# A build-time planner is told about the port that VectorE and GpSimd share, and two of its duration formulas are refitted

## What is computed

```python
def block(x):                                   # x: 2048 x 256
    q, k, v = split(layernorm(x) @ Wqkv.T + b)   # 8 query pairs, 4 key pairs, 4 values of 256
    p1 = softmax(causal(q[:, 0] @ k[:, 0].T * D**-0.5))
    p2 = softmax(causal(q[:, 1] @ k[:, 1].T * D**-0.5))
    o = (p1 - lam * p2) @ v
    o = o * rsqrt(mean(o * o) + eps) * subln_w * (1 - LAMBDA_INIT)
    x = x + layernorm(concat_heads(o) @ out_w.T + out_b)
    h = fwht(x * SU_ug) / 64
    h = silu(h @ W_gate.T * ws_g) * (h @ W_up.T * ws_u)
    return x + layernorm((fwht(h * SU_dp) / 64) @ W_down.T * ws_d)
```

## Time and profile before

| what | value |
|---|---|
| runs | 1252.57 us median of 3 (1249.90 to 1254.59) |
| profiled execution | 1250.54 us |
| its span, first to last instruction | 1248.7 us |
| busy PE / DVE / ACT / POOL | 1194.9 (96%) / 993.0 (80%) / 984.4 (79%) / 833.3 (67%) us |
| mean granted TensorE clock | 0.995 of full speed |

### The profile page before, as it was taken

One profiled execution on the slowest core, in us unless ns is written; L12 is line 12 of the kernel. 1 busy time (PEld: TensorE's weight loads), 2 busy tenths in 40 slices (PEclk: granted clock), 3 DMA queues, 4 the chain that ended last, 5 costly groups with the idle time before them and its releaser, 6 DMA issues.

```text
span 1248.7 us, 26399 instructions
## 1 busy us (share of the span) xinstructions
PE 1194.9 (96%) x8102; PEld 1010.6 (81%) x8102; DVE 993.0 (80%) x2492; ACT 984.4 (79%) x2617; POOL 833.3 (67%) x1167
## 2 busy tenths in 40 slices
PE   8899999999999999999999999999988899999998
PEld 7787888888878888888888888889777678777887
DVE  6888888888778988889689988887778899837445
ACT  4788988988789888888689889887887789856341
POOL 3576776666666776767577776566569887875542
PEclk9999999999999999999999999999999999999999
DMA  3255554463266556542555554543645455530001
GB/s 132 63 83 103 90 97 93 90 113 69 49 119 110 96 90 92 103 78 52 124 90 96 89 96 89 100 77 69 112 90 100 93 99 103 120 60 2 29 18 38
DMA packets 368153, 106.62 MB, mean 85 GB/s; under 512 B 359312, under 2 KB 365712, under 8 KB 367504
## 3 DMA queue, kind: packets, MB, share of 16 engines
q1 hardware_dynamic: 366672, 103.37, 44.4%
q10 hardware_dynamic: 1344, 1.57, 0.4%
HBM read 14.71 MB, written 2.10 MB: 13 GB/s over the span
## 4 chain that ended last, share of the span: by engine, by line
PE 49%; DVE 20%; POOL 11%; ACT 9%; issue 7%; DMA 3%; SPq 1%; ACTq 0%; POOLq 0%; DVEq 0%
PE score_bank L1181 6%; DVE p L1460 6%; PE score_bank L1047 5%; PE score_bank L1053 4%; DVE mx L1449 4%; PE score_bank L1050 4%; POOL e_all L1733 4%; ACT e_all L1220 4%; PE turn_bank L1074 2%; PE turn_bank L1076 2%; PE turn_bank L1075 2%; DVE score_bank L1444 2%; PE turn_bank L1091 2%; PE turn_bank L1127 2%; PE turn_bank L1146 2%
## 5 line engine op out<-in xcount | busy, mean ns | idle before, releaser
L1220 ACT ACTIVATE e_all<-score_bank,negmx 128x512 f32<-128x512 f32 (+2 forms) x640 | 395.4, 629 | 40.1 <-DVE negmx L1453 27.0
L1733 POOL TENSOR_TENSOR e_all<-e_all 128x512 f32<-128x512 f32 (+3 forms) x320 | 375.8, 1190 | 41.2 <-ACT e_all L1235 32.2
L1047 PE MATMUL score_bank<-k_hi,q_hi 128*128 128x512 f32 (+2 forms) x640 | 254.8, 398 | 27.2 <-ACT e_all L1220 16.3
L1460 DVE SCALAR_TENSOR_TENSOR p<-e_all,gain,p 128x512 f16<-128x512 f32 (+3 forms) x320 | 257.8, 821 | 17.6 <-ACT p L1242 17.3
L1449 DVE TENSOR_REDUCE mx<-score_bank 128x1 f32<-128x512 f32 (+1 forms) x384 | 242.1, 637 | 28.6 <-PE score_bank L1053 27.8
L1242 ACT ACTIVATE p<-e_all,gain 128x512 f16<-128x512 f32 (+3 forms) x320 | 206.8, 673 | 37.0 <-POOL e_all L1733 36.2
L1050 PE MATMUL score_bank<-k_lo,q_hi 128*128 128x512 f32 (+2 forms) x640 | 231.5, 362 | 0.4 <-DVE k_lo L1510 0.4
L1053 PE MATMUL score_bank<-k_hi,q_lo 128*128 128x512 f32 (+2 forms) x640 | 231.6, 362 | 0.0
L1784 POOL TENSOR_SCALAR ratio<-s,inv,neg_lam 128x1 f32<-128x1 f32 x128 | 55.9, 437 | 175.5 <-DVE inv L1721 175.0
L1047 PEld LDWEIGHTS score_bank<-k_hi,q_hi 128*128 128x128 f32 x640 | 120.8, 189 | 64.4 <-ACT e_all L1220 31.3
L1074 PE MATMUL turn_bank<-v,p16T 128*128 128x256 f16 x592 | 163.0, 275 | 0.0
(11 more groups left out here) (384 smaller groups left out, 2822.0 us busy)
## 6 DMA issues: line engine op xcount, KB each, us to landing
p16T<-p SPq DMA_TRANSPOSE x320, 3.1
w_raw<-in_w_qkv_dram SPq DMA_DIRECT2D x3, 1024.0 KB, 5.5
w_raw<-in_w_o_dram SPq DMA_DIRECT2D x4, 512.0 KB, 3.2
oT<-o SPq DMA_TRANSPOSE x128, 2.5
bv<-in_hidden_dram SPq DMA_DIRECT2D x8, 256.0 KB, 3.1
w_raw<-in_w_ug_dram SPq DMA_DIRECT2D x4, 512.0 KB, 3.6
out_dram<-e SPq DMA_DIRECT2D x16, 128.0 KB, 1.7
e<-in_w_d_dram SPq DMA_DIRECT2D x1, 1024.0 KB, 6.0
```

The lines of the kernel that those rows point to most:

```text
L1047: pe.matmul(bank[:, 0:w], qh, kh, start=True, stop=False)
L1220: act.activation(e, S[k % NS][:, 0:w], ACT.Exp, bias=negmx[:, d % 2, m, s:s + 1], scale=-1.0 if alone else 1.0, accum_out=ssum[:, d % 4, s ...
L1460: dve.scalar_tensor_tensor(out=halves_of(q, w)[1], in0=e1_of(q, w), scalar=gain[:, d % 4, s:s + 1], in1=halves_of(q, w)[0], op0=ALU.mult, ...
L1733: pool.tensor_tensor(a, a, b, ALU.add).then_inc(p_pool, 1)
```

## The change

In words, in the order of the diff:

1. PE durations in the plan. A score set of `w` columns goes from `0.00136 * w + 0.01` to `0.00135 * w + 0.003`; a product chunk from `0.00257 * w + 0.02` to `0.002555 * w`; the 0.083 us that the plan added to a score set behind a product or an output (`SWITCH_US`, with the list `ran`) is gone.
2. POOL durations. `MIX` goes from `0.19 + 0.00212 * w` to `0.22 + 0.00198 * w`, `VL` from 1.3 to 1.15.
3. A port in the simulation. `BOTH_FROM_SBUF` names the DVE steps that read two tensors from SBUF (the `SPLIT` of a chunk, weight splits, `FH`, `DB`); `LONG_ON_POOL` names the long POOL steps. A listed DVE step started while a long POOL step runs is charged the rest of that step; any POOL step started during a listed DVE step is charged the rest of that one.
4. A choice. A listed DVE step is left out of the candidates while the long POOL step that runs still needs 0.3 us or more (`HELD_SHORT`), unless it has been ready for over 6 us (`HELD_LONG`).
5. `FB` 0 to 3 may not start in the plan until SP's `WO` of the last group plus 5 us; SP's `FB` steps get a line of their own ("DF" for "D").
6. One instruction stream changes directly: ACT waits, ahead of `SQ` of tile `o`, for its own `SQ` of tile `o - 2`.

```diff
-LOAD_LAG, SWITCH_US, TURN_LAG = 0.16, 0.083, 2.9
-SCORE_US, VALUE_US = 0.00136, 0.00257
+LOAD_LAG, TURN_LAG = 0.16, 2.9
+SCORE_US, VALUE_US = 0.00135, 0.002555
+BOTH_FROM_SBUF = ("SPLIT", "WQ", "WK", "WV", "WO", "FH", "DB")
+LONG_ON_POOL = ("MIX", "VL", "FB", "NA", "HH", "DB")
+HELD_SHORT, HELD_LONG = 0.3, 6.0
...
-    ran = ["X"]
+    port, ready_at = {"DVE": 0.0, "POOL": 0.0}, {}
...
-                        add("M", "POOL", "MIX", (d, jj), 0.19 + 0.00212 * ww, [("POOL", "GAIN", o)], 2)
+                        add("M", "POOL", "MIX", (d, jj), 0.22 + 0.00198 * ww, [("POOL", "GAIN", o)], 2)
...
-            add("V", split, "VL", what, 0.75 if split == "DVE" else 1.3, [("ACT", "V", what)], 1)
+            add("V", split, "VL", what, 0.75 if split == "DVE" else 1.15, [("ACT", "V", what)], 1)
...
-            add("D", "SP", "WO", what, 0.3, [("DVE", kind, what)], 1)
+            add("D", "SP", "WO", what, 0.3, [("DVE", kind, what)], 1, 5.0)
...
-            loaded = [("SP", "FB", what // 2 * 2 - 3)] if what >= 4 else []
+            loaded = [("SP", "FB", what // 2 * 2 - 3)] if what >= 4 else [("SP", "WO", (GROUPS - 1, s)) for s in range(2)]
...
-            add("D", "SP", kind, what, 0.3, [("POOL", kind, what)], 1, 5.0 if what in (1, 3) else 0.0)
+            add("DF", "SP", kind, what, 0.3, [("POOL", kind, what)], 1, 5.0 if what in (1, 3) else 0.0)
...
-            return SCORE_US * duo_chunks(what[0])[what[1 + 1]][4] + 0.01
+            return SCORE_US * duo_chunks(what[0])[what[1 + 1]][4] + 0.003
         if kind == "PV":
-            return VALUE_US * duo_chunks(what[0])[what[1]][4] + 0.02
+            return VALUE_US * duo_chunks(what[0])[what[1]][4]
...
-                us = pe_us(kind, what) + (SWITCH_US if kind == "S" and ran[-1] in ("PV", "OP") else 0)
-                ran.append(kind)
+                us = pe_us(kind, what)
...
+        if engine == "DVE":
+            for _, _, op in heads:
+                if op.kind in BOTH_FROM_SBUF:
+                    ready_at.setdefault((op.kind, op.what), now[0])
+            heads = [x for x in heads if x[2].kind not in BOTH_FROM_SBUF or port["POOL"] - now[0] < HELD_SHORT
+                     or now[0] - ready_at[x[2].kind, x[2].what] > HELD_LONG]
...
+        if engine == "DVE" and op.kind in BOTH_FROM_SBUF:
+            us += max(0.0, port["POOL"] - now[0])
+            port["DVE"] = now[0] + us
+        elif engine == "POOL":
+            us += max(0.0, port["DVE"] - now[0])
+            if op.kind in LONG_ON_POOL:
+                port["POOL"] = now[0] + us
...
                         act.wait_ge(pv_done, last_part[o] + 1)
+                        if o >= 2:
+                            act.wait_ge(msq_ready, o - 1)
```

## The result

| | median | ratio to the kernel before, with 95% interval |
|---|---|---|
| before | 1253.58 us (6 runs) | |
| after | 1264.61 us (6 runs, 1260.99 to 1268.08) | 1.0093 [1.0073, 1.0114] |

The forecast was 1243.5 us with a range of 1232 to 1257: the time lies 7.6 us above the end of the range and moved the other way.

What follows compares the result with a forecast made beforehand. PE was taken as the bound, with only its idle time to win: 12.7 us won at score sets less 3.5 given back, net 9, takes the profiled 1250.54 us to 1241.5, the median to 1243.5; range 1232 to 1257.

Steps and rivals of the forecast that it cites:

- PE is the bound, and only its idle time moves: Whole kernel: no matmul goes away, so only PE's idle time can be won, 39.2 us of it in attention.
- 0 in the sum and 1.5 to either side: TensorE's clock, granted at 0.85 in 950 to 960 us: some 1.5 us of lost work that may go or return.
- PE's durations were 34 us too long in the plan: Old plan believed PE some 34 us slower than it is; corrected, it would place product chunks where PE stood.
- 12.7 us: Gain forecast at PE's score sets waiting for the exponential: half of 25.4 us of waits.
- The port's charge makes the plan truer, so it helps: In the plan: old one believes DVE 0.8 us per duo too fast, and POOL too; the new one charges both.
- A held SPLIT ends no later than a blocked one: On DVE: held or blocked, SPLIT starts when POOL is through; holding lets a ready maximum go first.
- The prediction's row at 502: At 502.56 us a DVE SPLIT started during a POOL MIX and took 1.34 us, against 0.75 alone.
- Given back by late SPLITs: 3.5 us, at most 9.3: Loss from late SPLITs, between 0 and about ACT's 9.3 us of waits for transposed room; 3.5 us taken.
- The third rival: Held SPLITs come too late for the rings: 20 us more ACT ring waits, PE loses 10 us; 1262 us, chance 0.11.
- the signs that it named: For the slow case: ACT's waits for transposed chunks grow beyond 25 us; DVE's idle time for ACT's SPLIT half grows.
- The first rival: Blocked DVE time becomes held time, nothing more: gain 0 to 4 us, time 1251 us, chance 0.24.
- The rival's sign: For blocked time merely becoming held: SPLIT and POOL step means fall, PE's score-set waits don't.

Runs made afterwards that it cites:

- fpe_pe_durations: The changed kernel with only PE's new durations: MIX and VL durations as before, no port charge, no hold; 1238.93 us, ratio 0.9872.
- f010_charge: The changed kernel with the old durations and no hold, so the port charge alone; 1257.24 us, ratio 1.0033.
- E2: Not a run: a scaling step of the kernel that the plan gives to ACT or POOL; it has no measured time of its own.
- g_base30: The changed kernel with old durations, no charge, no hold, and the planned transpose delay at 3.0 us instead of 2.9; 1266.60 us, ratio 1.0101.
- f101_dur_hold: The changed kernel with the port charge alone taken out, so all new durations and the hold; 1252.26 us, ratio 0.9996.
- h_rank1: The changed kernel, whole change included, with DVE's half of SPLIT at rank 1 in the plan instead of 2; 1240.18 us, ratio 0.9887.
- g_after28: The changed kernel, whole change included, with the planned transpose delay at 2.8 us instead of 2.9; 1250.74 us, ratio 0.9963.

## Why the prediction was wrong, by its own steps

*PE is the bound, and only its idle time moves.* Right as to the bound. The changed kernel's busy time did stay within 3 us of 1194.9, as forecast (1196.3), but only because two things cancel: 8.9 us less work at full speed and 10.3 us more by the clock. Not all of the time is in the idle rows: fpe_pe_durations is 14.4 us shorter in span than before, of which 5.8 us are idle time and 8.6 us are PE's busy time (1186.3 against 1194.9) at the same clock of 0.995. The ends of matmuls are modelled in the profile, so short waits may be hidden in busy time; that this is all of it was not shown.

*The clock, "0 in the sum and 1.5 to either side".* Mis-sized: on PE's work the clock took 10.3 us more than before, of a span that grew by 14.2. The prediction looked at one place of low clock in the kernel before and not at what new waits could do to it.

*PE's durations were 34 us too long in the plan, and correcting them wins.* Right as to the error: `plan()` adds up 1071.8 us for PE with the old durations and 1038.2 with the new. Right in sign as to the gain, and in size partly by luck: 12.7 us were forecast, all at score sets, and PE's durations alone won 13.6 us (1252.57 to 1238.93) and 1.1% in the second draw; but in fpe_pe_durations the waits at score sets fell by 5.6 us only (25.4 to 19.8), and the larger part lies in the busy time, which the prediction let stand. In the changed kernel itself 3.5 us were won at score sets instead of 12.7.

*The port's charge makes the plan truer, so it helps.* This is the step that failed. The prediction booked the charge on the side of the gain with no cost of its own. Measured, it costs 25 us on the plan with PE's durations (1238.93 to 1264.04), 12 us on the one with all new durations (1244.74 to 1256.31), as much again on the one that has these and the hold (1252.26 to 1264.61), and 4.5 us on the old one (1252.72 to 1257.24), the last within the scatter of draws. The reason lies, as far as the plans show it, in the rank rule. The list built by `plan()` gives way to a maximum (rank 0) whenever one is ready; the fuller DVE looks, the longer `SPLIT` (rank 2) gives way. With the charge DVE looks too full: the plan of f010_charge adds 109 us to 128 of the 320 `SPLIT`s, up to 2.03 us each (summed inside the plan), where that kernel's trace has 97 of them stretched by over 0.1 us, 53.5 us in sum (each duration less 742 ns for 512, 607 for 384 keys, 475 and 343 for the small ones). One source of the excess can be read in the code: if POOL also scales (`E2`), the plan holds the port over both instructions as one, while on the chip they are two. That this excess, and not the charge as such, makes the harm was not tried. That the lateness comes from DVE's side of the charge can be seen in the plans, which give the same "late" as the traces within 0.4 us. In the plan of f010_charge it is 2.5 us; with DVE's charge alone it would be 2.7, with POOL's alone 1.4, as in the plan before (no such kernel was run). In the changed kernel the hold keeps DVE's charge small, 22 us against 35.5 us of stretch in its trace. There DVE doesn't look too full; the hold does the passing over.

*A held SPLIT ends no later than a blocked one.* Right for one hold, wrong for the list. The prediction's row at 502 has `SPLIT` waiting for one `MIX`; but once passed over it stands behind maxima that PE hasn't computed yet, and on the chip DVE then waits for these with the `SPLIT` ready: 24.0 us, 0.3 before, as added up above. DVE's idle time before maxima grew by more than that; after:
```profile
DVE mx L1466 <- PE score_bank L1068: 47.2, 73, 2.6
DVE score_bank L1456 <- PE score_bank L1068: 37.6, 31, 3.1
...
DVE score_bank L1461 <- PE score_bank L1068: 28.3, 37, 3.2
```
That is 113.1 us in 141 waits; before, the same three (L1449, L1439, L1444) were 27.8, 15.8 and 12.8 us, 56.4 together. By itself this idle time is no sign of loss: in fpe_pe_durations, the fastest kernel, it is 67.6 us. What tells them apart is whether a `SPLIT` lay ready in it (0.4 us there).

*Given back by late SPLITs: 3.5 us, at most 9.3.* This is the term of the sum in which the failed step shows. The mechanism was named, its size was wrong: PE's direct waits for `p16T` grew by 15 us and ACT's from 9.3 to 21.1 us. The upper bound was taken from a row of before, where `SPLIT`s were early; a row can't bound a wait that the change itself creates. The third rival (1262 us, chance 0.11) described what happened and gave the time to 3 us, but it was argued down with "PE itself hardly stands at product chunks", which was true of the kernel before only. Its time was in part luck. It saw the path in ACT's waits for the ring; the larger part are PE's 11 direct waits for a chunk, and what the clock took was not in it. Of the signs that it named neither came: ACT's waits for `p16T` stayed under 25 us (21.1), and DVE's idle time for ACT's half of a `SPLIT` fell, from 17.3 to 3.3 us.

*The first rival, with the Trainium skill's "SBUF — State Buffer", section "Who interferes with whom".* Blocked time did fall (50.0 us of stretch before, 35.5 after, by the same sum), so far this case agrees with the rule that the two instructions exclude each other. The rival's sign came nearly so, too: the means fell, the waits at score sets hardly. But the time didn't stay at 1251 us, because the rule says nothing of what a list does with a step that is passed over.

*What was not in the prediction at all*: the kernel before is itself a lucky draw. Against the mean of its three draws (1.0062) the whole change is level (1.0040); the draws lie between 1.0006 and 1.0101 before and between 0.9963 and 1.0093 after. So the measured 0.93% is, in part, luck of one order against another. What held in the draws that were made: PE's durations win 1.7% against their partners (mean of 0.9872 and 0.9889 against mean of 1.0006 and 1.0101), the whole change, which adds charge and hold (and the new `MIX` and `VL`), gives nearly all of it back, and an earlier rank of `SPLIT` returns it, twice.

*Where the loss is not shown.* On the old durations the charge (1.0033), the hold (1.0014) and both (1.0015) are no slower than the mean of the three draws of the plan before, though `SPLIT` is late there as well (2.2 to 3.0 us) and PE waits for `p16T` for 7.9 to 15.9 us. And the slowest kernel of all, g_base30, has early `SPLIT`s (1.1 us); it lost at score sets (30.1 us, 25.4 before). So a late `SPLIT` is shown to cost time on plans with PE's durations corrected, and it is one way of several to lose 1%.

Open: why these kernels with the old durations are no slower than before with so much waiting for `p16T`, and why PE's busy time at full speed falls by 9 us with the new ones. On one draw each, single cells of the table can't be told from the scatter.

## What to carry to other kernels

A truer duration can make a static plan worse through its priority rule: if one engine looks fuller, or holds a step back, whatever has the low rank becomes late, and the bill comes one engine further on. PE's truer durations needed no such care; the charge and the hold did. Read how long the low-ranked step lies ready before it is taken up, before and after: here 1.2 and 3.0 us. And before one plan is judged against another, draw each two or three times with a constant that means nothing; here that alone moved the ratio by 0.95% on the plan before and by 1.3% on the changed one, as much as the change did or more. The kernel to keep is fpe_pe_durations at 1238.93 us (0.9872), or the whole change with `SPLIT` at rank 1 at 1240.18 (0.9887), which was drawn twice as well.

## What the runs showed of the hardware

That a `SPLIT` on DVE that starts during a `MIX` on POOL ends late was in the rows of before already (1.34 us against 0.75 alone). Not expected was how little this blocked time says of the whole: over all orders the number of `SPLIT`s stretched by over 0.1 us lies between 58 and 108 of 320. f101_dur_hold has the least (58, 31.3 us) and is no faster than the kernel before; fpe_pe_durations has 103 (53.3 us) and is the fastest; h_rank1, the next, has 62 (33.2 us).

Nor was it expected how much of a loss comes by the clock. One kernel, g_after28, took between 1241.72 us (mean granted clock 0.994) and 1253.51 us (0.986) in ten executions; the four under 1246 us have 0.991 or more, the six over 1250 us 0.989 or less. A wait of PE can thus be paid twice, once as idle time and, as behind the wait until 1057.53, once more by the clock after it. How much can't be read from PE's idle time alone: g_base30 has 64.9 us of it and loses 6.8 us of work to the clock, the changed kernel 66.6 and 15.4.
